# First attention of a macaron stack: projections split by ScalarE and GpSimd instead of VectorE, with another timetable for the side work

## The reference, cut to what matters

```python
qkv = x @ Wqkv.T
q, k, v = jnp.split(qkv, 3, axis=-1)
q, k, v = map(merge_heads, (q, k, v))
dots = jnp.einsum('bhid,bhjd->bhij', q, k) * dh ** (-0.5)
dots = jnp.where(causal_mask, -jnp.inf, dots)
attn = jax.nn.softmax(dots, axis=-1)
out = jnp.einsum('bhij,bhjd->bhid', attn, v)
out = out.transpose(0, 2, 1, 3).reshape(b, t, d)
return out @ Wout.T + bout
```

## Time and profile before

| | |
|---|---|
| median of three timed runs | 1815.1 us |
| profiled execution, its own time | 1809.93 us |
| span from first to last instruction | 1808.0 us |
| TensorE busy, share of the span | 84% |
| VectorE | 66% |
| ScalarE | 54% |
| GpSimd | 38% |
| mean granted TensorE clock | 0.922 of full speed |

### The profile page before, as it was taken

How to read it: one execution, slowest core, us unless ns; L and a number is a source line. 1 busy time by engine, 2 the same in 40 slices (tenths; PEclk the granted TensorE clock), 3 DMA queues, 4 the chain that set the end, 5 groups by cost and what they waited for, 6 DMA issues and landing times. The chain is left out here.

```text
span 1808.0 us, 35347 instructions
## 1 busy us (share of the span) xinstructions
PE 1524.2 (84%) x12511; PEld 1008.8 (56%) x12511; DVE 1199.7 (66%) x2260; ACT 971.2 (54%) x1727; POOL 690.6 (38%) x1145
## 2 busy tenths in 40 slices
PE   6999966999999999998799896456888889888874
PEld 5568853544443444434666785234666667676653
DVE  6635558588888888883754565656566777766434
ACT  3324432377777777775343442323677667667641
POOL 0687743011111111111088764342244454453432
PEclk9999988599999999998699998677999999999987
DMA  7122521011111111110513242100000000000000
GB/s 257 35 78 75 148 84 32 20 35 27 27 39 27 36 30 34 27 26 7 208 42 92 85 131 79 52 0 1 2 2 2 5 8 5 5 8 9 7 4 13
DMA packets 49469, 81.52 MB, mean 45 GB/s; under 512 B 10868, under 2 KB 34868, under 8 KB 48628
## 3 DMA queue, kind: packets, MB, share of 16 engines
q1 hardware_dynamic: 40212, 60.50, 11.5%
q0 software_dynamic: 9088, 18.76, 3.1%
HBM read 43.18 MB, written 31.22 MB: 41 GB/s over the span
## 5 line engine op out<-in xcount | busy, mean ns | idle before, releaser
L1979 DVE TENSOR_REDUCE z_parts<-z_pS 128x8 f32<-128x1024 f32 (+1 forms) x320 | 350.5, 1115 | 51.4 <-PE z_pS L1712 33.4
L1894 ACT ACTIVATE z_Pr<-z_pS 128x1024 f32<-128x1024 f32 (+1 forms) x320 | 297.5, 940 | 121.2 <-PE z_pS L1736 120.6
L2083 POOL TENSOR_SCALAR_AFFINE_SELECT z_Pr<-z_Pr 128x512 f32<-128x512 f32 x128 | 80.8, 637 | 445.5 <-ACT z_Pr L1894 445.5
L356 POOL DMA_INDIRECT slot_results<-m_yq,m_xq x156 | 153.9, 987 | 75.6 <-ACT m_yq L561 45.3
L332 POOL DMA_INDIRECT slot_rows<-m_XN,m_dest x128 | 129.9, 1015 | 93.7 <-DVE m_dest L650 58.3
L1750 PE MATMUL z_pO<-z_Pr,z_V 128*9 128x512 f32 (+3 forms) x1536 | 160.2, 489 | 3.1 <-ACT z_oT L1881 1.6
L1736 PE MATMUL z_pS<-z_QM,z_QK 64*128 64x512 f32 (+1 forms) x640 | 150.4, 470 | 1.4 <-DVE z_parts L1979 0.2
L1736 PEld LDWEIGHTS z_pS<-z_QM,z_QK 64*128 64x128 f32 x640 | 59.7, 185 | 155.4 <-issue 111.6
L1712 PE MATMUL z_pS<-z_KM,z_Q 64*128 64x512 f32 (+1 forms) x640 | 133.2, 414 | 15.1 <-ACT z_Pr L1894 14.7
L974 PE MATMUL f_gup<-s_wguT,f_xT 128*128 128x352 f32 x234 | 97.7, 501 | 34.2 <-DVE f_src L1281 19.0
L705 DVE TENSOR_TENSOR m_h<-m_sg,m_gu 128x512 f32<-128x512 f32 x78 | 53.7, 688 | 90.9 <-ACT m_sg L553 90.8
(11 more groups left out here) (296 smaller groups left out, 3852.3 us busy)
## 6 DMA issues: line engine op xcount, KB each, us to landing
slot_rows<-in_c_pad SPq DMA_DIRECT2D x2, 5070.0 KB, 24.9
m_xq<-slot_rows SPq DMA_DIRECT2D x38, 260.0 KB, 4.3
z_KM<-z_QK SPq DMA_DIRECT2D x60, 128.0 KB, 2.4
z_QM<-z_Q SPq DMA_DIRECT2D x128, 48.0 KB
m_raw<-in_gu SPq DMA_DIRECT2D x2, 2048.0 KB, 9.1
m_XN<-slot_results SPq DMA_DIRECT2D x8, 512.0 KB, 4.1
m_raw<-slot_results SPq DMA_DIRECT2D x8, 512.0 KB, 5.5
slot_results<-m_yq,m_xq POOLq DMA_INDIRECT x156
```

The lines of the kernel that those rows point to most:

```text
L356: g_.indirect_dma_start(y_dram, bass.IndirectOffsetOnAxis(xq[q % RING][:, j % QT, TAG[list_of(j)]:TAG[list_of(j)] + 1].bitcast(I32), 0), y ...
L1894: a.activation(Pr[j % 4][:, :, q * P:(q + width) * P], heads(G, EXPONENTIAL, e)[:, :, 0:width * P], ACT.Exp, scale=DH0 ** -0.5).then_inc(e ...
L1979: v.tensor_reduce(parts[:, qt, kb:kb + width, :].rearrange("p t h -> p h t"), b.rearrange("p h (t k) -> p h t k", k=P), AX.X, ALU.max).the ...
L2083: g_.affine_select(blk, blk, [[0, 4], [1, P]], ALU.is_ge, 0.0, base=0, channel_multiplier=-1).then_inc(selected, 1)
```

## The change

- Each of the four projection pieces of groups 2 to 15 is now split by ScalarE and GpSimd. `keep_both` on ScalarE writes two tiles: `high`, now already multiplied by the 0/-1 column (`scale` added to the instruction), and a new tile `whole`, a plain copy. GpSimd adds the two into `Q` or `QK`. VectorE's main loop has no split. The pieces of groups 0 and 1 are made as before.
- TensorE frees `pX` on `high_done` (ScalarE done) and not on `split_done`. GpSimd's list is now by step, with splits ahead of the masking of the same step.
- The timetable moves: projections from steps 3, 9, 13, 17 to 4, 10, 16, 18 and in the order keys, keys, queries, queries; `AT_V`, `AT_TAKE`, `AT_O1`, `AT_FIN`, `AT_O0`, `AT_M0`, `AT_MAX` as shown. SyncE's waits follow the new order.

```diff
-        high = s.sb("high", [P, 512], F32R)
+        high, whole = s.sb("high", [P, 512], F32R), s.sb("whole", [P, 512])
...
-        AT_V = (5, 6, 7, 8, 10, 12, 14, 16, 18, 20, 21, 22)
-        AT_TAKE = (9, 3)
-        AT_M1, AT_O1, AT_FIN, AT_O0, AT_M0 = 2, 5, (7, 8), 11, 15
-        Q_LOW, K_LOW, K_HIGH, Q_HIGH = 2, 0, 1, 3
-        AT_PROJECT = (3, 9, 13, 17)
-        ORDER = (Q_LOW, K_LOW, K_HIGH, Q_HIGH)
+        AT_V = (5, 7, 8, 9, 11, 13, 15, 17, 19, 20, 21, 22)
+        AT_TAKE = (10, 3)
+        AT_M1, AT_O1, AT_FIN, AT_O0, AT_M0 = 2, 6, (8, 9), 12, 14
+        K_LOW, K_HIGH, Q_LOW, Q_HIGH = 0, 1, 2, 3
+        AT_PROJECT = (4, 10, 16, 18)
+        ORDER = (K_LOW, K_HIGH, Q_LOW, Q_HIGH)
...
-        AT_MAX = 7
+        AT_MAX = 9
...
-                        sp.wait_ge(split_done, 4 * (G + 2) + 3)
+                        sp.wait_ge(split_done, 4 * (G + 2) + 2)
...
+                def keep_both(G, i, k):
+                    need(act, proj_done, 4 * G + k + 1)
+                    need(act, split_done, 4 * G + k)
+                    a.activation(high[:, :], pX[:, :], ACT.Identity, bias=rows[:, 1 - i // 2:2 - i // 2], scale=rows[:, 3 - i // 2:4 - i // 2])
+                    a.activation(whole[:, :], pX[:, :], ACT.Copy).then_inc(high_done, 1)
...
-                            keep_high(G + 2, ORDER[AT_PROJECT.index(e)], AT_PROJECT.index(e))
+                            keep_both(G + 2, ORDER[AT_PROJECT.index(e)], AT_PROJECT.index(e))
...
-                        for k in range(4):
-                            if n == AT_PROJECT[k] + 1 and further:
-                                split(G + 2, ORDER[k], k)
...
+                def split(G, i, k):
+                    pool.wait_ge(high_done, 4 * G + k + 1)
+                    need(pool, st_ready, NE * (G - 2) + (NE0 if i % 2 else 0) + 1 if i // 2 else NE * (G - RING + 1))
+                    dst = Q[G % 2] if i // 2 else QK[G % RING]
+                    g_.tensor_tensor(dst[:, (i % 2) * 512:(i % 2) * 512 + 512], high[:, :].bitcast(F32), whole[:, :], ALU.add).then_inc(split_done, 1)
...
-                    for c in range(4):
-                        select(G, c, c)
-                    for c in range(4):
-                        select(G, 8 + c, c)
+                    for e in range(NE):
+                        if e in AT_PROJECT and G + 2 < NG:
+                            split(G + 2, ORDER[AT_PROJECT.index(e)], AT_PROJECT.index(e))
+                        j = EU[e][0]
+                        if e == FIRST_OF[j] and not 4 <= j < 8:
+                            select(G, j, j % 4)
```

More of the change, by code:

```diff
@@ L1605, in spread_keys @@
                         sp.dma_start(KM[G % 2][r, h % 2, c].bitcast(F32), QK[G % RING][r, c].bitcast(F32)).then_inc(done, 16)
-                QUERY_SPLITS = lambda G, half: 4 * G + (4 if half else 2 if G == 0 else 3 if G == 1 else 1)
+                QUERY_SPLITS = lambda G, half: 4 * G + (4 if half else 2 if G == 0 else 3)
                 def spread_queries(G, half):
@@ L1771, in main @@
                         if e == AT_M1:
-                            need(pe, split_done, min(4 * (G + 2), 4 * NG))
+                            need(pe, high_done, min(4 * (G + 2), 4 * NG))
                             need(pe, m_kept, 2 * G + 1)
@@ L1776, in main @@
                             need(pe, m_kept, 2 * G + 2)
-                            project(G + 2, Q_LOW)
+                            project(G + 2, K_LOW)
                         if e == AT_O1 and G > 0:
-                            need(pe, *((split_done, 4 * (G + 2) + 1) if further else (m_kept, 2 * G + 2)))
+                            need(pe, *((high_done, 4 * (G + 2) + 1) if further else (m_kept, 2 * G + 2)))
                             turn_output(G - 1, 1)
@@ L1785, in main @@
                         if e == AT_PROJECT[1] and further:
-                            need(pe, split_done, 4 * (G + 2) + 1)
+                            need(pe, high_done, 4 * (G + 2) + 1)
                             need(pe, o_normed, 2 * G)
@@ L1789, in main @@
                                 need(pe, fin_kept, 2 * (G // 4))
-                            project(G + 2, K_LOW)
+                            project(G + 2, K_HIGH)
                         if e == AT_O0:
[L1792 to L1795, removed]
+                            need(pe, *((high_done, 4 * (G + 2) + 2) if further else (o_normed, 2 * G)))
                             turn_output(G, 0)
+                        if e == AT_M0 and more:
+                            need(pe, o_normed, 2 * G + 1)
+                            turn_maximum(G + 1, 0)
                         if e == AT_PROJECT[2] and further:
[L1798 to L1805, removed]
+                            need(pe, m_kept, 2 * G + 3)
+                            project(G + 2, Q_LOW)
                         if e == AT_PROJECT[3] and further:
-                            need(pe, m_kept, 2 * G + 3)
+                            need(pe, high_done, 4 * (G + 2) + 3)
                             project(G + 2, Q_HIGH)
@@ L2006, in main @@
                 def main(G):
-                    more, further = G + 1 < NG, G + 2 < NG
+                    more = G + 1 < NG
                     for n in range(NM + 1):
```

## The result

The changed kernel takes 1823.2 us (median of six runs), the kernel before 1807.9 us beside it: the ratio is 1.0076, 95% interval 1.0045 to 1.0107. On another chip the same pair gave 1.0058 (1.0027 to 1.0089). So the change costs 0.6 to 0.8%: more than I forecast (no difference), inside the stated range of 1800 to 1830 us, and clear of zero.

A forecast was written before the change was run, and what follows sets the result against it. TensorE's ordered list, about 29.9 us per group, plus some 1.4 us of stalls was taken as the bound. Terms -0.14 - 0.86 + 0.30 + 0.36 + 0.30 + 0.11 = +0.07 us, times 14 = +1.0, gave 1816.1 us; range 1800 to 1830.

The forecast's parts named there:

- the 0.14 us at E 19: TensorE's late job in step 19 waits for VectorE's maximum of step 18; without splits, a gain of 0.14 us per group.
- M 5: TensorE's matmul job of step 5 waits for step 3's exponential; the new layout removes this delay, -0.86 us.
- M 6: TensorE's matmul job of step 6 waits for the longer exponential of projection step 4: stall 0.17 us.
- M 10: TensorE's matmul job of step 10 waits because moved value products leave too little work after step 8: stall 0.28 us.
- M 12: TensorE's matmul job of step 12 waits for the longer exponential of projection step 10: stall 0.06 us.
- M 13: TensorE's matmul job of step 13 waits after step 11, thinned by moved value products, despite turn_output between: stall 0.08 us.
- M 18: TensorE's matmul job of step 18 waits for the half-width exponential of projection step 16: stall 0.07 us.
- M 0: TensorE's first matmul job of the next group waits for GpSimd's last addition: stall 0.47 us instead of 0.36, +0.11.
- Rival 2: GpSimd's addition is stretched to 1.98 us, holding the next group's first matmul 0.93 us more: +13 us, 1829 us; chance 0.12.
- The seams: TensorE's jobs in steps 4, 6 and 12 lose shorter distances to neighbouring jobs: +0.3 us per group, between 0 and 0.5.
- Rival 1: Thin steps and seams cost nothing, or VectorE's lead feeds back: -1.1 us per group, -15 us, 1800 us; chance 0.22.
- Rival 3: ScalarE's backlog from step 10 is carried on: +0.8 us per group, +11 us, 1827 us; chance 0.06.

The follow-up runs named there:

- plan_only: The changed kernel's new timetable with the old engines (all four pieces split by ScalarE and VectorE): a group took 30.74 us, ratio to the kernel before 0.9969.
- add_twice_first_two: The changed kernel with GpSimd's addition made twice for the first two pieces of each group (steps 4 and 10): 31.87 to 31.91 us per group.
- fill_steps_4_19: The kernel before with only value products 0 and 9 moved, to steps 4 and 19: a group took 30.45 us, ratio to before 0.9942.
- the one experiment aimed at part (1): The kernel before with value products 0 and 9 in steps 4 and 19, AT_MAX 9, turn_maximum in step 1, value product 10 in step 2: ratio 0.991.
- add_twice_last: The changed kernel with GpSimd's last addition of each group (step 18) made twice: one full-clock group took 33.1 us, others up to 35.0.
- engines_only: The old timetable with the new engines (ScalarE writes two tiles, GpSimd adds): a group took 32.8 us, ratio to the kernel before 1.0127.

## Why the prediction was right or wrong, point by point

**What bounds the kernel: right.** TensorE's ordered list plus named waits set the group. Taking 3 us of work from VectorE gave back only what I had said, the 0.14 us at E 19; plan_only and add_twice_first_two show the rest as cover. VectorE ends a wait worth naming only once TensorE's other waits are gone (fill_steps_4_19), and there for 0.44 us.

**The waits: right in place, and in size but for one.** Measured as distance from E to the next M, beyond the 0.22 or 0.34 us that TensorE needs: M 5 went from 0.86 to 0 (forecast the same), M 6 is 0.16 (0.17), M 10 0.28 (0.28), M 12 0.01 (0.06), M 13 0 (0.08), M 18 0.06 (0.07). M 0 went from 0.36 to 0.61; I had 0.47. The step that failed there is the addition's duration: 1.28 us instead of 1.05, partly offset by the 0.05 us from its end to M 0 where I had 0.15. I had chosen as "nearest row" an instruction with broadcast operands. Rival 2 was this mechanism, a slower addition at the end of the path, but the runs speak against a stretch by neighbours: all 56 additions, at four different steps, take 1.27 to 1.29 us.

**The seams: wrong, outside my bounds.** I gave +0.3 us for less favourable neighbours on TensorE, between 0 and 0.5. What is left of the measured +0.64 us after all the waits (-0.22, counting 0.12 us of small waits of before at M 8, M 11 and M 16 that I had passed over) and the VectorE term (-0.14) is about +1.0 us. Read off both timelines of group 3, distance by distance, it falls into three parts. (1) What follows a diagonal matmul: before, four of the eight were followed by a pX job after 0.15 to 0.23 us; now all eight are followed by a value product or by E after 0.32 us, as at 465.96 above: 0.5 us. A projection behind a diagonal matmul in the kernel before:

```profile
446.39 0.39 PE L1716 MATMUL z_pS<-k_after_query,k_identb 128*128 128x256 bf16 x2
446.54 0.48 PE L1662 MATMUL z_pX<-s_xh,s_wh 128*128 128x512 f32 x1
```

(2) What follows an M: after an M of 512 columns that an exponential had released, even where that delayed it by 0.01 us or less, the next job starts 0.41 to 0.44 us later instead of 0.32 or 0.33, which is the distance behind the M at 471.31 in the earlier trace rows that hadn't waited; the change has five such places and the kernel before three; and the one place where E stood right behind M after 0.23 us is gone: together 0.3 us. M 6 of the changed kernel and the turn behind it:

```profile
445.44 0.50 PE L1712 MATMUL z_pS<-z_KM,z_Q 64*128 64x512 f32 x2
445.87 0.66 PE L1757 MATMUL z_pX<-k_ident,z_oT 128*128 128x128 f32 x4
```

(3) The turns of outputs take 0.59 instead of 0.53 us in their new place, 0.1 us for two. The account is made from the traces, and it closes for plan_only too: waits 1.0 us less than before, VectorE's 0.14 gone, measured -0.5, so about +0.6 for the seams, where the three parts give 0.5 + 0 + 0.1 (one job fewer is late behind an M there, which pays for the lost place of 0.23 us). That the distances add up is shown; the one experiment aimed at part (1) was spoilt by another wait, so why a job starts early or late behind a diagonal matmul stays open. The difference between my sum and the result comes mostly from here.

**Sum of it.** Forecast +0.07 us per group, measured +0.64: +0.7 from the seams, +0.14 from the addition at M 0, -0.27 from small waits that were smaller or vanished. The term that was mis-sized is thus the seams' +0.3, which measured about +1.0. That put the group at 31.89 us, above the 31.0 to 31.6 that I had given as the sign of being right. In engines: the new timetable gained 0.5 us, ScalarE's second copy lost 0.8 us with its waits and restarts, GpSimd lost 0.3 us. Each copy's direct wait was in the sum, but not that every wait, however short, adds a restart of 0.1 us.

That the time still fell into the stated range is partly luck. The forecast stood on a median of 1815.1 us for the kernel before, and six runs give 1807.9. As a difference of medians the change costs 15.3 us, against a forecast of 1.0, own bounds of -6 to +8, and a wide range that reached to about +15.

Group 14 was forecast at nothing and lost 0.9 us: 29.37 in plan_only too, so it is the timetable's, which leaves steps 4, 10, 16 and 18 empty where no projection fills them.

**Rivals.** Rival 1 (the stalls really go) failed, and rightly for the reason given: only one E in the group had stood at a maximum's end. Rival 3 (ScalarE's backlog is carried on) failed: the exponential behind step 10's row of three copies is on time again one step later, and M 12 waits 0.01 us.

## What to carry to other kernels

Where one engine's ordered list sets the time, work taken from another engine is worth only the waits which that engine ends last; look those up before weighing loads. Look instead for steps in which the limiting engine has nothing to do while it waits, and move a job there: two numbers in a timetable and a third for the wait that comes up next gave 0.9%, where moving 3 us of VectorE's work per group to other engines lost 0.7% with a new timetable and 1.3% with the old one. When work is moved to a slower engine, what matters is whether its last piece has a reader close behind: a second addition cost nothing at steps 4 and 10 and its full length at step 18.

## What the runs showed of the hardware

- A matmul job behind an M that had to wait starts 0.1 us late (0.41 to 0.44 us after M instead of 0.33, or 0.32 instead of 0.21 behind an M of 256 columns), even where M was held up by 0.01 us or less. In groups 1 to 15 of the kernel before, 55 M's with a job other than E behind them start less than 0.08 us after an exponential has ended, and behind all 55 the job is late; of the other 206 it is late behind 13, each time M 0, which had waited too. In the changed kernel it is 81 of 81, and again only the waiting M 0's of the other 193. Short waits cost more than their length.
- Two small instructions of VectorE's final maximum (128x16, from SBUF to SBUF) take 0.18 to 0.19 us alone, but one that starts while a GpSimd instruction is under way ends just after it does, 0.03 to 0.05 us. In the changed kernel GpSimd masks twice in a row from 467.99 to 469.22, and the two rows of VectorE's timeline are these; in the kernel before, where the CAST starts about 0.08 us before the end of a masking, the same instructions took 0.18 and 0.19.

```profile
468.06 0.60 DVE L1990 CAST z_mw<-z_m 128x16 fp32r<-128x16 f32 x1
468.70 0.56 DVE L1992 TENSOR_TENSOR z_mw<-z_m,z_mw 128x16 fp32r<-128x16 f32 x1
```

  It doesn't take GpSimd's addition: in plan_only the CAST is 0.56 us long in 14 groups, beside a masking. Nor is it a share of something, but the whole rest of GpSimd's instruction: in add_twice_last the CAST starts 0.07 us after an addition of 1.26 us and takes 1.23.

```profile
502.26 1.26 POOL L2091 TENSOR_TENSOR z_Q<-z_high,z_whole 128x512 fp32r<-128x512 f32 x1
...
502.33 1.23 DVE L1990 CAST z_mw<-z_m 128x16 fp32r<-128x16 f32 x1
```

  VectorE's maxima, which read PSUM, aren't lengthened by GpSimd (1.23 us for 128x1024 with and without it), and neither is the reduction just ahead of the CAST, which reads SBUF (0.38 us beside an addition, 0.37 alone). In the changed kernel no job of TensorE waits for the two that are. This is what the Trainium skill, "GPSIMD Engine Reference", section "8. Key points", calls shared SBUF interfaces, with contention for VectorE instructions in a two-port mode or with two SBUF inputs. The TENSOR_TENSOR row has two such inputs and agrees. The CAST has one and is held up as long; whether it ran in a two-port mode no row shows.
- A wait of 1.7 us once per group went with stretches at the lower clock in the loop (mean 0.94 in four groups, 0.96 to 1.00 in others), where a wait of 0.45 us (the changed kernel) and one of 1.38 us (engines_only) left groups 1 to 14 at 1.00.
